# A linear-attention stage whose order of work becomes a written table, with most of its constant products cut

## The reference

```python
xx = xprev - x                                    # x: after the layer norm
mix_in = tanh((x + xx * time_maa_x) @ time_maa_w1)
xrg, xwa, xk, xv = (x + xx * (maa_f + mix_f) for f in range(4))      # four small products
r = xrg @ w_receptance.T;  k = xk @ w_key.T;  v = xv @ w_value.T
w = -softplus(-(time_decay + tanh(xwa @ time_decay_w1) @ time_decay_w2)) - 0.5
g = tanh(xrg @ gate_w1) @ gate_w2
kk = normalised per head (k + tanh(xk @ kkk_w1) @ kkk_w2);  a, ma, mk2 = three sigmoids
def step(S, inp):                                 # a = -kk, b = kk * a
    sa = einsum('bhij,bhj->bhi', S, at)
    S = S * dt[:, :, None, :] + sa[..., None] * bt[:, :, None, :] + vt[..., None] * kt[:, :, None, :]
    return S, einsum('bhij,bhj->bhi', S, rt)
y = group norm of the outputs * ln_w + ln_b + (r * k * time_faaaa).sum(head) * v
out = y * g @ w_output.T
```

## Time and profile before

| | us |
|---|---|
| median of 3 runs | 3933.3 |
| lowest and highest | 3921.72, 3956.56 |
| the profiled execution, its own time | 3952.22 |
| span of its trace | 3950.5 |
| stage C in it, about | 1767 to 3515 |
| scans L2151, first and last start of 16 | 1813.7, 3314.0 |

### The profile page before, as it was taken

One profiled execution on the slowest core, in us unless ns is written; L12 is line 12 of the kernel. 1 busy time (PEld: TensorE's weight loads), 2 busy tenths in 40 slices (PEclk: granted clock), 3 DMA queues, 4 the chain that ended last, 5 costly groups with the idle time before them and its releaser, 6 DMA issues.

```text
span 3950.5 us, 118220 instructions
## 1 busy us (share of the span) xinstructions
PE 3216.3 (81%) x52210; PEld 2079.4 (53%) x52210; DVE 2545.8 (64%) x5294; ACT 1802.8 (46%) x3051; POOL 1035.9 (26%) x1164
## 2 busy tenths in 40 slices
PE   6989999987488989866788887877878877769995
PEld 4555555553255555533455555554545545547874
DVE  4665666665588888865666666655566655347775
ACT  3443444435378878843333333333333333226652
POOL 1331221223311212122122223222222122115552
PEclk7888998998699999987888888887888887769997
DMA  2229997000334343220000000000000000026666
GB/s 79 87 81 389 394 393 129 1 1 26 130 129 140 120 154 121 93 65 2 3 9 9 9 9 9 9 8 8 8 8 7 6 9 9 13 105 221 223 220 181
DMA packets 161680, 356.96 MB, mean 90 GB/s; under 512 B 13821, under 2 KB 98559, under 8 KB 154896
## 3 DMA queue, kind: packets, MB, share of 16 engines
q1 hardware_dynamic: 147088, 323.95, 24.1%
q0 software_dynamic: 14080, 25.45, 1.9%
HBM read 136.33 MB, written 216.67 MB: 89 GB/s over the span
## 4 chain that ended last, share of the span: by engine, by line
PE 53%; DVE 22%; ACT 13%; issue 7%; DMA 2%; another core or an unknown queue 1%; SPq 1%; POOL 1%; DVEq 0%; POOLq 0%; ACTq 0%
PE ps L1589 7%; PE ps L135 4%; PE ps L137 3%; PE ps L136 3%; DVE t L485 3%; PE ps L1654 3%; PE ps L1584 3%; PE ps L896 2%; PE ps L342 2%; ACT t L1035 2%; ACT t L1033 2%; PE ps L346 2%; PE ps L903 2%; PE ps L298 1%; PE ps L304 1%
## 5 line engine op out<-in xcount | busy, mean ns | idle before, releaser
L1589 PE MATMUL ps<-t 128*128 128x512 f32 x608 | 376.1, 735 | 41.9 <-ACT t L1914 12.9
L241 POOL TENSOR_SCALAR_AFFINE_SELECT t<-t 128x512 f32<-128x512 f32 x256 | 169.0, 661 | 662.2 <-ACT t L425 662.2
L485 DVE TENSOR_REDUCE t<-ps 128x2 f32<-128x512 f32 (+1 forms) x512 | 260.7, 551 | 119.7 <-PE ps L304 119.5
L135 PE MATMUL ps<-t 128*128 128x512 f32 (+1 forms) x660 | 280.1, 424 | 59.1 <-DVE t L511 34.4
L425 ACT ACTIVATE t<-ps 128x768 f32<-128x768 f32 x256 | 206.8, 808 | 215.1 <-PE ps L330 215.1
L137 PE MATMUL ps<-t 128*128 128x512 f32 (+1 forms) x660 | 258.2, 391 | 0.0
L136 PE MATMUL ps<-t 128*128 128x512 f32 (+1 forms) x660 | 258.0, 391 | 0.0
L1361 POOL DMA_INDIRECT deltas<-t x92 | 94.4, 1026 | 511.6 <-DVE t L1307 489.8
L2225 DVE COPY_PREDICATED t<-t,ps 128x128 f32<-128x128 uint32 x384 | 131.5, 342 | 147.3 <-PE ps L1654 80.3
L1584 PE MATMUL ps<-t 128*128 128x256 f32 (+1 forms) x544 | 207.7, 470 | 15.7 <-DVE t L2271 7.0
L2832 POOL DMA_INDIRECT answers<-t x156 | 153.9, 987 | 160.1 <-DVE t L2803 122.2
(11 more groups left out here) (443 smaller groups left out, 8586.4 us busy)
## 6 DMA issues: line engine op xcount, KB each, us to landing
paired<-t SPq DMA_DIRECT2D x14, 8384.0 KB, 59.9
t<-experts SPq DMA_DIRECT2D x39, 1536.0 KB
sorted<-t SPq DMA_DIRECT2D x22, 1950.0 KB, 8.8
t<-in_wP SPq DMA_DIRECT2D x92, 320.5 KB, 3.5
experts<-t SPq DMA_DIRECT2D x8, 1536.0 KB, 6.0
t<-sorted SPq DMA_DIRECT2D x39, 260.0 KB
t<-answers SPq DMA_DIRECT2D x16, 512.0 KB, 6.7
t<-in_wE SPq DMA_DIRECT2D x8, 768.0 KB, 7.5
```

The source lines that it names most:

```text
L135: pe.e.matmul(out, a[0], b[0], start=start, stop=False, skip_group_check=True)
L241: pool.e.affine_select(own, own, [[0, 2], [0, 2], [1, 128]], ALU.is_ge, 0.0, base=0, channel_multiplier=-1).then_inc(*kept(b, j))
L485: m = dve.e.tensor_reduce(nmf[:, z, blk * 16 + 4 * g + i0:blk * 16 + 4 * g + i0 + 2], ps[:, k:k + 2, a0:a1], AX.X, ALU.max, negate=True)
L1589: pe.e.matmul(ps[out, k, :], lhs, rhs, start=True, stop=True).then_inc(*e_pe(u, name))
```

## The change

`steps_c` no longer decides anything: a table `AT` gives each of the 138 steps of a unit a place, unit u is moved by 138 u places, and the steps are sorted by place. Seen modulo 138, every place is taken once. A unit's steps stretch from -243 to 346, so that four to five units are under way at once. `HOLD` gives the width of each constant product by tile or state step; most are 0 now, and none is issued then: 17 products of 3840 columns a unit become 7 of 1536 (128 in one tile's step 2, 384 in one tile's step 9, and 384, 128, 128, 256, 128 in five of six state steps). Since the first E step of a unit now stands between steps of the unit before, its wait is for a later event of that unit ("k" instead of "xn"), because both use the same buffer.

```diff
-HALFWAY = 5
-STEPS = {"E": 29, "L": 17, "I": 10, "S": 35}
-PACE = {"E": 0.9, "L": 1.05, "S": 1.05}
-WRITTEN = 16
+UNIT = 138
+AT = {"E": (-243, -236, -219, -216, -208, -198, -188, -183, -179, -170, -162, -151, -147, -138, -136, -133, -132,
...
+HOLD = {"tp": (0, 0, 128, 0), "bd": (384, 0, 0, 0), "s": (384, 128, 128, 256, 128, 0),
+        "fc": 0, "rl": 0, "rk": 0}
...
 def steps_c():
...
-        if k < 64 and (not active or (len(active) == 1 and begun[active[0]] >= HALFWAY)):
...
-            for name in lanes:
-                pace[name] = min(pace[name] + PACE[name], 1.0 + PACE[name])
-                while pace[name] >= 1 and ready(name):
-                    yield advance(name)
-                    pace[name] -= 1
+    steps = []
+    for u in range(16):
+        steps += [(UNIT * u + at, ("E", u, n)) for n, at in enumerate(AT["E"])]
+        steps += [(UNIT * u + at, ("S", u, n)) for n, at in enumerate(AT["S"])]
+        for half in range(2):
+            steps += [(UNIT * u + at, ("L", u, half, n)) for n, at in enumerate(AT["L"][half])]
+        for tile in range(4):
+            steps += [(UNIT * u + at, ("I", 4 * u + tile, n)) for n, at in enumerate(AT["I"][tile])]
+    for _, step in sorted(steps):
+        yield step
...
         def hold(k, n):
-
-            pe.e.matmul(ps[:, k, 0:n], w["bones"], w["reset"][:, 0:n], start=True, stop=True, skip_group_check=True)
+            if n:
+                pe.e.matmul(ps[:, k, 0:n], w["bones"], w["reset"][:, 0:n], start=True, stop=True, skip_group_check=True)
...
-                hold(b, 128)
+                hold(b, HOLD["tp"][tile])
...
-                hold(b, 256)
+                hold(b, HOLD["bd"][tile])
...
-                    hold(k, 256)
+                    hold(k, HOLD["s"][s])
...
                 if u:
-                    dve.wait_ge(e_dve, u - 1, "xn")
+                    dve.wait_ge(e_dve, u - 1, "k")
```

More of the change, by code:

```diff
@@ L1430 @@
 HS = (16, 8, 4, 2, 1)
-HALFWAY = 5
-STEPS = {"E": 29, "L": 17, "I": 10, "S": 35}
-PACE = {"E": 0.9, "L": 1.05, "S": 1.05}
-WRITTEN = 16
-def steps_c():
[L1440 to L1474, removed]
-        if k < 64 and (not active or (len(active) == 1 and begun[active[0]] >= HALFWAY)):
-            while ("L", k // 4, k % 4 // 2) not in done:
-                for name in ("L", "E", "S"):
-                    if ready(name):
-                        yield advance(name)
[L1480 to L1487, removed]
-            for name in lanes:
-                pace[name] = min(pace[name] + PACE[name], 1.0 + PACE[name])
-                while pace[name] >= 1 and ready(name):
-                    yield advance(name)
-                    pace[name] -= 1
-    while lanes["S"]:
-        yield advance("S")
@@ L1786, in state @@
                 pe.wait_ge(*misc.free("fc", u))
-                hold(k, 256)
+                hold(k, HOLD["fc"])
                 pe.wait_ge(s_dve, u, "rk")
@@ L1818, in state @@
                 pe.wait_ge(*misc.free("rl", u))
-                hold(k, 256)
+                hold(k, HOLD["rl"])
                 pe.e.matmul(ps[:, k, 0:32], w["ones"], w["cbias"], start=True, stop=False, skip_group_check=True)
@@ L1833, in state @@
                 pe.wait_ge(*misc.free("rk", u))
-                hold(k, 256)
+                hold(k, HOLD["rk"])
                 pe.wait_ge(r_dve, u, "prior")
```

## The result

The changed kernel takes 3623.2 us (median of 4 runs, 3622.0 to 3635.6) beside 3938.9 us: 0.9205 of the time, with a 95% interval of 0.9158 to 0.9253. Repeated on three other occasions, the ratio was 0.9212, 0.9212 and 0.9229.

The account below looks back on a forecast made before the run. PE bounds the kernel, a fifth of its time idle. Per unit, 100 - 4.3 (constant products) - 8.7 (waits) + 0.2 (tables) + 0 (clock) = 87.2 us; with -5 at the end, -197 us: 3736 us, range 3640 to 3860.

Parts of the forecast that it names:

- The first rival: Stage C: almost all PE waits go, clock 0.93 instead of 0.84; unit 79.3 us, time 3618 us; chance 0.13.
- issue: PE idle in stage C with no cause named by the trace: 6.0 us a unit, expected to stay.
- the clock, set to 0: PE's clock in stage C's steady part: stays at 0.84 with PE busy 84% instead of 80%, so 0.
- The waits: PE's waits for other engines in stage C: steps placed further apart take 8.7 of 13.8 us a unit.
- The rank term: Rank product's wait for DVE's chain: 29 places instead of 13, 1.7 of 2.0 us a unit go.
- the doublings: Second doubling's wait for ScalarE's copy: steps 4 and 5 further apart, 3.4 of 3.9 us a unit go.
- the state term: State steps' waits: first one 19 places on instead of 3, steps 3 and 4 close; 0.9 of 2.1 us go.
- The constant products: Fewer constant products on PE: 7.3 us of work a unit go, of which 4.3 us is time gained.
- the slower rival: Middle of each unit: without constant products the clock falls; at 0.55, unit 108.3 us, time 4053 us; chance 0.04.
- The tables of ScalarE: ScalarE in stage C: 59 table loads instead of 47, 1283 ns each; +0.2 us a unit.
- Head and end: Stage C outside its steady part: nothing at the head, -5 us at the end from narrower constant products.

Follow-up runs that it names:

- order_alone_3: The changed kernel's order of steps with all 17 constant products a unit of the kernel before: 3663.1 us, 0.9265 of the kernel before.
- after_3: The changed kernel itself, run again beside the kernel before: 3643.6 us, 0.9212 of it.
- table_no_const_3: The changed kernel with no constant product at all: 3641.7 us, 0.9209 of the kernel before.
- before_3: The kernel before, unchanged, profiled on the same occasion: 3942.9 us.

## Why the prediction was wrong

**The bound and the mechanism were right**: PE was the bound, the distances in the table took away its waits, and DVE, now at 74%, did not take their place. The first rival (almost all waits go and the clock rises) gave 79.3 us a unit and 3618 us; measured are 79.7 and 3623. Its chance of 0.13 was too small, and its number was in part luck, by two errors that nearly cancel: it had waits and "issue" together fall by 10.8 us a unit, where they fell by 7.4, and the busy time by 9.9, where it fell by 13.0.

**The step that failed is the clock, set to 0.** The argument was that PE's busy share would go from 80% to 84% and that this leaves the clock where it is. The share came out as forecast, 84% (67.2 of 79.7), and the clock rose from 0.84 to 0.93 all the same, so the share was the wrong thing to read it from. By the order alone it went from 0.85 to 0.93, with 8.2 us a unit less busy time for the same products. In the first pair of profiles the forecast's busy time, 80.2 - 7.3 = 72.9 us a unit, was 67.2, and its idle time, 87.2 - 72.9 = 14.3, was 12.6: of the 7.5 us by which the unit was forecast too long, 5.7 are busy time, though no product had gone but the constant ones. The traces had a hint: the falls of the clock in the trace of before all stood behind idle time, and the forecast took two thirds of PE's waits for other engines away without asking what they had brought with them. Why exactly the clock rose stays open between fewer idle times and what work fills the time.

**The waits**, -8.7 us a unit, were -11.7 by the order alone and -9.7 in the first pair of profiles: right mechanism, sized a quarter too low. The rank term held (2.0 us to 0.1), the doublings too (their wait is gone), and the state term, for which 0.9 was taken because steps 3 and 4 of S stay close, was nearer to 1.5 (32.2 us of such waits in 15 units before, 9.6 after).

**The constant products**, -4.3, measured -1.7 in the new order and 0 in the old (there at the lower level only). The work they cost was right (12.1 and 4.8 forecast, 12.5 and 4.9 measured), but not all of it held PE: 4.6 us of the 6.6 that go from order_alone_3 to after_3. What they gave back was not in the sum: in the new order it is cover of waits for 1.1 us, as the term had it, but for 1.8 the clock at which the others run. So the rule cited for the slower rival was at work, at a price of most of what the products cost: from order_alone_3 to table_no_const_3 they take 8.3 us of PE's time with them, and the unit loses 1.5.

**"issue"**, left standing at 6.0, grew to 8.3: 2.3 us a unit lost that the sum did not have. It was let stand without a reason, and it rose with the new order.

**The tables of ScalarE**: 59 loads of 1283 ns, as forecast; no wait of PE behind one is among the rows, and 0.2 can't be told from 0. **Head and end**, -5: the stage is 1741.3 us in before_3 and 1435.5 in after_3, 305.8 less, of which 15 units are 292; so -14.

In sum, in the profiles of one occasion: waits -10.5, the busy time of products other than constant ones -5.6, constant ones alone -5.4, issue +2.1: -19.4 a unit. The forecast had -12.8.

## What to carry to other kernels

Where a list of steps sets the order on all engines at once, a distance can be worth more than the wait it removes, that between a product and the product that needs another engine's copy or sum of it. Here 11.7 us of waits a unit went, and with them 8.2 us of busy time, because the same products ran at 0.93 of the clock instead of 0.85. So count the busy time twice, at the clock before and at a clock that may come after. Constant products gained nothing here in either order; all of them together cost 0.6 to 1.1% in the new one, far less than their own length, so take them out last and measure. And in a ring of banks a moved step changes whose bank it takes: look for the wait that appears there before judging the move.

## What was not expected of the hardware

**PE's nameless idle time looks like the loading of its instructions.** It comes inside groups of products that have no wait in them, as here in the changed kernel, 1.79 us between two products of one loop:

```profile
2002.04 0.28 PE L1616 MATMUL ps<-t 64*32 64x32 f32 x12
2004.11 0.61 PE L1616 MATMUL ps<-t 64*32 64x32 f32 x50 [1.79 <-issue]
```

In the changed kernel's steady part the queues of the DMA engines show

```profile
q0 software_dynamic: 3584, 7.46, 1.9%
q8 instruction: 274, 4.49, 1.6%
```

274 packets of instructions, 4.49 MB, beside PE's 34,772 + 34,760 records: 64.6 bytes a record and 254 records a packet. Counted in the trace, nearly all pauses of over 0.8 us inside a loop (60 in the changed kernel's steady part) are a multiple of about 255 records apart. The Trainium skill (Advanced Engine Details and Errata, "ISA Cache") has lines of 16 KB for 256 instructions, which agrees. PE has more of it where it waits less for others: 6.0 us a unit before, 8.3 after. No run here removed PE instructions, so the cause is argued, not shown; if it holds, it is the largest idle time that is left.

**The kernel before has two levels of time**, 3844 and 3939 us, by the occasion and not by the run; three kernels with the table that were run at both differ by 49 to 72 us. The profiles of these three pairs show where. Of 59, 82 and 74 us between the spans of their profiled executions, 44, 53 and 50 lie in this stage, and 15, 29 and 25 in the stages ahead of it; behind it the spans agree (435.9 to 437.8 us in every profile). In the steady part "issue" is 1.1 to 1.4 us a unit shorter at the lower level, and busy time 0.7 to 1.5, at a clock 0.01 or 0.02 higher; waits for other engines differ by 0.5 or less. Of the kernel before there is no profile at the lower level, but the clock over its whole executions is 0.887 and 0.889 there and 0.879 at the higher one. What makes the difference stays open.
